# The attention state of an LSTM scan: tanh before the transpose instead of behind it

## The reference

```
def step(carry, x_t):
    h0, c0, h1, c1, a = carry
    xin = jnp.concatenate([x_t, a], axis=-1)
    h0, c0 = _lstm_cell(xin, h0, c0, Wi0, Wh0, bi0, bh0)
    h1, c1 = _lstm_cell(h0, h1, c1, Wi1, Wh1, bi1, bh1)
    q = h1 @ Wq.T
    attn = jax.nn.softmax(jnp.einsum('bh,bsh->bs', q, context), axis=-1)
    mixed = jnp.einsum('bs,bsh->bh', attn, context)
    a2 = jnp.tanh(jnp.concatenate([mixed, h1], axis=-1) @ Wo.T + bo)
    return ((h0, c0, h1, c1, a2), a2)
```

## Time and profile before

| | us |
|---|---|
| median of 3 runs | 8549.0 |
| lowest, highest | 8542.76, 8554.08 |
| the profiled execution, its own time | 8551.91 |
| its span (first to last instruction) | 8550.1 |

### The profile page before, as it was taken

One profiled execution on the slowest core, in us unless ns is written; L12 is line 12 of the kernel. 1 busy time (PEld: TensorE's weight loads), 2 busy tenths in 40 slices (PEclk: granted clock), 3 DMA queues, 4 the chain that ended last, 5 costly groups with the idle time before them and its releaser, 6 DMA issues. The chain is left out here.

```text
span 8550.1 us, 813808 instructions
## 1 busy us (share of the span) xinstructions
PE 6854.1 (80%) x380497; PEld 5819.4 (68%) x380505; DVE 4292.8 (50%) x21168; ACT 3215.7 (38%) x15021; POOL 279.5 (3%) x289
## 2 busy tenths in 40 slices
PE   6888888888888888888888888888888888576677
PEld 5777777777777777777777777777777777353455
DVE  5554555454555454555454555454555454556812
ACT  3333333333333333333333333333333333323322
POOL 0000000000000000000000000000000000113411
PEclk8999999999999999999999999999999999798788
DMA  1000000000000000000000000000000000000233
GB/s 54 0 0 0 0 0 0 0 0 0 0 0 0 0 0 0 0 0 0 0 0 0 0 0 0 0 0 0 0 0 0 0 0 0 25 12 11 105 118 112
DMA packets 62275, 93.29 MB, mean 11 GB/s; under 512 B 13984, under 2 KB 50848, under 8 KB 61344
## 3 DMA queue, kind: packets, MB, share of 16 engines
q1 hardware_dynamic: 59168, 84.45, 2.9%
q0 software_dynamic: 3072, 8.39, 0.3%
HBM read 73.94 MB, written 18.87 MB: 11 GB/s over the span
## 5 line engine op out<-in xcount | busy, mean ns | idle before, releaser
L302 PE MATMUL scan_sums<-rec_wh,scan_hT 128*4 128x64 f32 x131008 | 2391.8, 219 | 3.4 <-issue 3.4
L423 DVE STREAM_TRANSPOSE scan_sums<-scan_sums 128x64 f32<-128x64 f32 x6144 | 1545.7, 266 | 1141.4 <-PE scan_sums L302 1141.3
L302 PEld LDWEIGHTS scan_sums<-rec_wh,scan_hT 128*4 128x4 f32 x131008 | 1989.2, 88 | 3.7 <-issue 3.7
L302 PE MATMUL scan_sums<-rec_wa,scan_aT 128*4 128x64 f32 (+1 forms) x65536 | 1103.5, 219 | 383.4 <-ACT scan_aT L383 382.3
L302 PEld LDWEIGHTS scan_sums<-rec_wa,scan_aT 128*4 128x4 f32 (+1 forms) x65536 | 914.5, 88 | 572.2 <-ACT scan_aT L383 570.8
L302 PE MATMUL scan_sums<-rec_wx,scan_xT 128*4 128x64 f32 (+1 forms) x65536 | 1291.0, 219 | 2.5 <-issue 1.6
L302 PE MATMUL scan_sums<-rec_wi,scan_hT 128*4 128x64 f32 (+1 forms) x65536 | 1103.0, 219 | 167.3 <-DVE scan_hT L437 165.8
L302 PEld LDWEIGHTS scan_sums<-rec_wi,scan_hT 128*4 128x4 f32 (+1 forms) x65536 | 913.7, 88 | 356.4 <-DVE scan_hT L437 354.8
L302 PEld LDWEIGHTS scan_sums<-rec_wx,scan_xT 128*4 128x4 f32 (+1 forms) x65536 | 1023.6, 89 | 2.8 <-issue 1.7
L363 ACT ACTIVATE scan_sums<-rec_bias 128x192 f32<-128x192 f32 x2050 | 687.1, 335 | 475.8 <-DVE scan_hT L437 470.1
L368 ACT ACTIVATE scan_tanh_f<-scan_sums 128x8 f32<-128x8 f32 x2048 | 364.1, 178 | 1190.5 <-DVE scan_sums L423 1190.5
(11 more groups left out here) (253 smaller groups left out, 5843.7 us busy)
## 6 DMA issues: line engine op xcount, KB each, us to landing
experts_bias<-in_b SPq DMA_DIRECT2D x40, 640.0 KB, 3.8
moe_w<-in_w SPq DMA_DIRECT2D x16, 1024.0 KB, 12.5
slots_x<-route_zero SPq DMA_DIRECT2D x40, 128.0 KB, 1.7
experts_x<-slots_x SPq DMA_DIRECT2D x40, 128.0 KB, 2.1
slots_y<-experts_y SPq DMA_DIRECT2D x40, 128.0 KB, 1.7
front_x<-in_x_steps SPq DMA_DIRECT2D x32, 128.0 KB, 2.0
w_xres<-in_x SPq DMA_DIRECT2D x4, 1024.0 KB, 9.8
out<-w_xres SPq DMA_DIRECT2D x8, 512.0 KB, 3.0
```

Source lines behind the costliest of these rows:

```text
L302: last = nc.tensor.matmul(sums[layer][BANK[g]][32 * j:32 * j + ROWS[g], 0:64], state[:, k, FIRST[g]:FIRST[g] + ROWS[g]], weight[:, k, j, 6 ...
L423: nc.vector.transpose(turned[l][g], sums[l][g][:, 0:64]).then_inc(gates_turned[l][g], 1)
```

## The change

The tanh and the transpose change places. ScalarE now reads `a_sum` in its natural layout, all 64 columns on 128 partitions, as soon as the products have ended, and writes `a_natural` in SBUF. VectorE waits for that (`a_made`), turns `a_natural` and writes the state's tile `aT` directly; its transpose releases `a_ready`. For this `aT` becomes one row of B + 64 = 68 columns, the turned 64 from column 4 on. The weight loads of `wa`'s products take their 4 or 8 columns from it at 32k, and the copy into the history reads the used columns of the same tile.

```
-        a_sumT = a_sum[:, 128:192]
+        aT = m.sbuf("aT", [P, B + 64])
+        a_turned = aT[:, B:B + 64]
+        a_state = a_turned.rearrange("p (k u) -> p k u", k=2)[:, :, 0:B]
...
-        aT = m.sbuf("aT", [P, 2, 3 * B])
+        a_natural = m.sbuf("a_natural", [P, 64])
...
+                def of_state(state, k, first, rows):
+                    if state is aT:
+                        return state[:, 32 * k + first:32 * k + first + rows]
+                    return state[:, k, first:first + rows]
...
-                                                        state[:, k, FIRST[g]:FIRST[g] + ROWS[g]],
+                                                        of_state(state, k, FIRST[g], ROWS[g]),
...
                 def make_a(n):
-                    act.wait_ge(a_turned, n)
-                    nc.scalar.activation(state_of(aT), a_sumT.rearrange("p (k u) -> p k u", k=2)[:, :, 0:B], ACT.Tanh).then_inc(a_ready, 1)
+                    act.wait_ge(a_summed, n)
+                    nc.scalar.activation(a_natural[:], a_sum[:, 0:64], ACT.Tanh).then_inc(a_made, 1)
...
-                    dve.wait_ge(a_summed, n)
-                    nc.vector.transpose(a_sumT, a_sum[:, 0:64]).then_inc(a_turned, 1)
+                    dve.wait_ge(a_made, n)
+                    nc.vector.transpose(a_turned, a_natural[:]).then_inc(a_ready, 1)
                     dve.wait_ge(a_ready, n + 1)
-                    nc.vector.tensor_scalar(a_hist[:, bass.ds(t + s, 1), :, :].rearrange("p t k b -> p (t k) b"), state_of(aT),
+                    nc.vector.tensor_scalar(a_hist[:, bass.ds(t + s, 1), :, :].rearrange("p t k b -> p (t k) b"), a_state,
```

More of the change, by code:

```diff
@@ L288, in scan @@
                                                        for n in ("f_tanh", "c_terms", "c_done", "h_factors", "h_ready"))
-        (a_ready, x_ready, scores_done, max_done, exps_done, p_turned, probs_ready, a_summed, inv_done, a_turned, a_kept, zeroed) = (
+        (a_ready, x_ready, scores_done, max_done, exps_done, p_turned, probs_ready, a_summed, inv_done, a_made, a_kept, zeroed) = (
             m.sem(n) for n in ("a_ready", "x_ready", "scores_done", "max_done", "exps_done", "p_turned", "probs_ready", "a_summed",
-                               "inv_done", "a_turned", "a_kept", "zeroed"))
+                               "inv_done", "a_made", "a_kept", "zeroed"))
         opened = m.sem("opened")
```

## The result

The changed kernel takes 8579.54 us in the median of 7 runs (8574.8 to 8580.94), and the kernel before took 8551.95 us in 7 runs beside them (8542.76 to 8556.64). The ratio is 1.0033, with a 95% interval of 1.0023 to 1.0043. So it is slower, by 28 us, and by more than the 0.2% that this kernel's measurements can tell. The forecast was 8554 us and no change that can be told; it was wrong.

A forecast was written before the change was run, and what follows sets the result against it. A bare chain between recurrence steps was taken to bound the kernel; transpose -40, tanh +47 and handoffs -2 and 0 gave +5 ns a step, +5 us, so 8554 us, with 8532 to 8580 to hold 8 times in 10.

The forecast's parts named there:

- What bounds the step: Border between two recurrence steps: a bare chain from products to weight load, each ns counting 1024 times, 1.02 us in total.
- The transpose, -40 ns: State's transpose on VectorE, now between SBUF tiles: 226 ns like the exponentials' row, against 266 from PSUM to PSUM.
- The tanh, +47 ns: State's tanh on ScalarE, from 2x4 columns to 64, PSUM to SBUF: from 178 to 225 ns.
- The straight line and the subtraction of the bias tile: Two ways to the 64-column tanh: 225 ns between rows of 8 and 256 columns; 317 - 90 = 227 ns.
- The handoffs, -2 and 0: Waits between engines in the link: ScalarE to VectorE -2 ns; VectorE to weight load and TensorE to ScalarE 0 each.
- C: TensorE's handoff to ScalarE is shorter, ScalarE starting 0.03 us sooner: step 25 ns shorter, 8523 us; chance 0.10.
- D: TensorE's handoff to ScalarE is longer, 0.13 us: +70 ns, +75 a step, 8626 us; chance 0.05.
- A: The 64-column tanh has a foot of its own, 238 ns, +60 instead of +47: 8567 us; chance 0.12.
- B: The tanh costs what the exponential of 65 columns costs, 317 ns, +139: 8648 us; chance 0.03.
- The work beside the link: Beside the products-to-weight-load chain: ScalarE's take_x moving earlier and VectorE's history copy waiting on its own semaphore cost 0.
- The sum: Whole link: -40 + 47 - 2 + 0 = +5 ns a step, +5 us over 1024 steps.
- the transpose's other bound: State's transpose gains 0 ns, staying at 266, if memory wasn't what made the slow row slow: kernel +46 us.

The follow-up runs named there:

- six kernels: The changed kernel, four variants of it and one variant of the kernel before; measured ratios 1.0033, 1.0030, 1.0032, 1.0019, 1.0025 and 0.9975.
- the narrow version: Changed kernel with the tanh of 8 columns of the sum instead of 64, the transpose still turning all 64: 8523.68 us, ratio 0.9975.

## Why the prediction was wrong

*What bounds the step* was right. The border is a bare chain, and what its durations gained or lost reached the time one for one within the intervals, in six kernels.

*The transpose, -40 ns,* is the step that failed. The text said that the trace "has just that operation in that shape", and that is so; but the row is of a transpose that starts behind a reciprocal that still runs, until 3000.19 + 0.17 = 3000.36:

```profile
3000.19 0.17 DVE L442 RECIPROCAL scan_inv<-scan_scores 128x1 f32<-128x1 f32 x1 [0.45 <-ACT scan_exps L378]
3000.28 0.23 DVE L444 STREAM_TRANSPOSE scan_expsT<-scan_exps 128x64 f32<-128x64 f32 x1
```

Half of the 40 ns between the two rows is the memory, which the change does bring, and half is the start behind the running reciprocal, which it doesn't bring, since the state's transpose waits for ScalarE on an idle VectorE. The forecast took the whole for the memory. The term measured -21. With -21 in place of -40 the forecast's own sum gives +24 ns, which is what came. The bounds were -40 and 0, so the value was inside them, and I chose the end. A sign of it stood in the view by line: the exponentials' transpose has 0.0 us of idle time ahead of it, and the state's must have its wait there.

*The tanh, +47 ns,* was right: 224 ns, +46. The straight line and the subtraction of the bias tile both held, and the narrow version's 177 ns at 8 columns shows the slope again (47 ns for 56 columns, 0.84 each). By the Trainium skill's page "ScalarE: Activation LUTs" (section "What ACT_TABLE_LOAD costs") the estimate was 239 ns. The trace has 224, and the measurement decides.

*The handoffs, -2 and 0,* were right within what the timelines can show; by the idle time of the weight loads they came to nothing together. ScalarE starts 3003.65 - 3003.59 = 0.06 us behind the products' modelled end, VectorE about 0.03 behind the tanh, and the weight load 0.055 behind the transpose (0.052 before). Rivals C and D, with 0.03 and 0.13 us for the first of these, are refuted by it.

*The rivals.* A came nearest in the time (8567 us, +18 us), but its mechanism, a tanh of 238 ns, isn't there: right side, wrong term. B is refuted by the 224 ns.

*The work beside the link* cost nothing, as said: take_x can stand in either place (1.0030 and 1.0032), and the copy didn't delay the gate.

*The sum.* +5 was forecast and +25 came; of the 20 ns that are missing 19 are the transpose's. The range held the time, 8579.54 under 8580, by half a microsecond. That was luck: the range reached so far for A's sake, whose mechanism wasn't there. The chances didn't hold it: 0.20 stood on slower. I had given the transpose's other bound no case of its own, though the text named it (+46 us); a case at half of it was the true one.

## What to carry to other kernels

A duration in a profile belongs to an instruction in its surroundings: before a row is used as the price of another, see whether its engine was idle ahead of it, and take it only for an instruction that will start in the same way, or give the difference a bound and a case of its own. In a latency-bound loop a swap of two operations moves both durations through their width and their memories; add these up from rows, since nothing hid the error here. Where two rows differ in two ways, the difference isn't the price of either.

## What the runs showed of the hardware

- VectorE's fp32 transpose of 128x64, from an idle engine: 245 ns between SBUF tiles, 249 PSUM to SBUF, 259 SBUF to PSUM, 265 PSUM to PSUM. Between SBUF tiles it takes 211 at 32 columns and 311 at 128. Starts of the output at columns 0 to 16 and of the input at 0 to 8 change nothing (245 to 247).
- Right behind a running reciprocal the same rows read 224 to 246, about 20 ns less each, and 203 behind another transpose. In the recurrence, though, the third gate's transpose, from PSUM to PSUM, starts only some 0.05 us behind L431 and takes at least 265 ns like the others. Which property of the instruction ahead decides this stays open.
- ScalarE's tanh: 177 or 178 ns for 8 columns from PSUM to SBUF and 224 for 64; 162 and 208 from PSUM to PSUM; 208 for 2x4 columns from SBUF to SBUF. Writing PSUM instead of SBUF saves 16 ns at either width, and reading SBUF costs 30 more at 2x4 columns. A copy of 2x4 columns between SBUF tiles takes 192 where nothing of ScalarE runs beside it.
